# Scan of a two-block transformer kernel: local attention products as block-diagonal matmuls, values for two head pairs at a time

## What is computed

```
scores = einsum('bhnd,bhmd->bhnm', q_s, k_s) * SCALE          # rotated q, k
scores = where(mask, scores, -inf)
sdpa   = einsum('bhnm,bhmd->bhnd', softmax(scores), v_s)      # local products
num    = einsum('bhnk,bhkv->bhnv', elu1(qn_s), mem); den = ...
out    = beta * num / (den + 1e-6) + (1 - beta) * sdpa
prev_v = einsum(elu1(kn_s), mem) / ...
mem    = mem + einsum('bhnk,bhnv->bhkv', elu1(kn_s), v_s - prev_v)
```

## Time and profile before

| | us |
|---|---|
| three runs, median (lowest to highest) | 3109.3 (3105.91 to 3112.54) |
| the profiled execution, own time | 3109.39 |
| its span in the profile | 3107.6 |
| PE busy of the span | 2664.5 (86%) |
| DVE busy | 2506.4 (81%) |
| ACT busy | 1875.9 (60%) |
| POOL busy | 1758.7 (57%) |
| scan, 1700 to the end | 1407 |

### The profile page before, as it was taken

How to read it: one execution, slowest core, us unless ns; L and a number is a source line. 1 busy time by engine, 2 the same in 40 slices (tenths; PEclk the granted TensorE clock), 3 DMA queues, 4 the chain that set the end, 5 groups by cost and what they waited for, 6 DMA issues and landing times. The chain is left out here.

```text
span 3107.6 us, 129631 instructions
## 1 busy us (share of the span) xinstructions
PE 2664.5 (86%) x53553; PEld 1513.6 (49%) x53553; DVE 2506.4 (81%) x7598; ACT 1875.9 (60%) x3797; POOL 1758.7 (57%) x1988
## 2 busy tenths in 40 slices
PE   5887999999999999782331899999999998999998
PEld 2442333333333333372220666666666666666665
DVE  4677989999999999586606888888888888888887
ACT  5785999999999999630001555555455555555543
POOL 5883222222222222240063888888888888888886
PEclk9896999999999999895655999999999999999999
DMA  4676434444444443191023000000000000000000
GB/s 126 205 241 155 90 89 94 94 107 94 91 94 98 96 94 87 39 325 55 10 40 91 4 11 11 11 11 4 11 11 11 11 11 11 11 11 5 11 8 11
DMA packets 173633, 201.58 MB, mean 65 GB/s; under 512 B 31152, under 2 KB 134512, under 8 KB 172784
## 3 DMA queue, kind: packets, MB, share of 16 engines
q1 hardware_dynamic: 170480, 191.87, 23.8%
q0 software_dynamic: 2560, 1.35, 0.4%
HBM read 125.10 MB, written 67.24 MB: 62 GB/s over the span
## 5 line engine op out<-in xcount | busy, mean ns | idle before, releaser
L851 ACT ACTIVATE at_pA<-at_ps 128x512 f32<-128x512 f32 x1024 | 551.8, 614 | 57.8 <-DVE at_ps L903 51.1
L912 DVE CUSTOM_DVE_ANT_0 at_junk<-at_ps,w_cmask 128x512 f32<-128x512 f32 (+3 forms) x1024 | 463.4, 485 | 102.7 <-PE at_ps L754 95.4
L903 DVE TENSOR_TENSOR at_ps<-at_ps,w_ratio 128x128 f32<-128x128 f32 (+3 forms) x1024 | 451.2, 491 | 2.1 <-PE at_ps L748 0.5
L720 POOL TENSOR_SCALAR_AFFINE_SELECT at_pB<-at_pB 128x128 f32<-128x128 f32 x256 | 74.8, 292 | 640.4 <-ACT at_pB L857 638.3
L857 ACT ACTIVATE at_pB<-at_ps 128x512 f32<-128x512 f32 (+1 forms) x768 | 379.5, 531 | 53.0 <-PE at_ps L761 47.7
L2001 POOL TENSOR_TENSOR sc_rb<-sc_rb,v_sin 128x512 f32<-128x512 f32 x256 | 326.0, 1274 | 42.4 <-DVE sc_ra L2241 41.1
L2037 PE MATMUL sc_ps<-sc_xT,v_wqkv 128*128 128x512 f32 x512 | 287.2, 644 | 4.0 <-PEq L56 1.4
L748 PE MATMUL at_ps<-at_aq,at_ak 72*128 72x512 bf16 x1024 | 278.3, 388 | 0.2
L2200 ACT COPY sc_skN<-sc_ps 128x512 f32<-128x512 f32 x128 | 75.1, 587 | 324.8 <-PE sc_ps L2089 324.8
L1996 POOL TENSOR_TENSOR sc_sk<-sc_ee,sc_relu 128x512 f32<-128x512 f32 x128 | 165.4, 1293 | 180.8 <-ACT sc_ee L2191 180.7
L761 PE MATMUL at_ps<-at_bq,at_bk 75*128 75x512 bf16 (+3 forms) x1024 | 265.8, 302 | 1.5 <-ACT at_pB L857 0.9
(11 more groups left out here) (317 smaller groups left out, 5949.9 us busy)
## 6 DMA issues: line engine op xcount, KB each, us to landing
parts_scratch<-fr_parts SPq DMA_DIRECT2D x64, 384.0 KB, 4.1
at_bk<-parts_scratch SPq DMA_DIRECT2D x192, 96.0 KB
at_ak<-parts_scratch SPq DMA_DIRECT2D x192, 96.0 KB
v_scratch<-fr_v SPq DMA_DIRECT2D x32, 352.0 KB, 4.4
at_v<-v_scratch SPq DMA_DIRECT2D x32, 352.0 KB, 3.5
at_bq<-parts_scratch SPq DMA_DIRECT2D x128, 64.0 KB
at_aq<-parts_scratch SPq DMA_DIRECT2D x128, 64.0 KB
on_scratch<-at_on SPq DMA_DIRECT2D x32, 256.0 KB, 2.2
```

The lines of the kernel that those rows point to most:

```text
L851: act.activation(pA[:, n % A_RING, j * S:(j + 1) * S], src, ACT.Exp).then_inc(exped, 1)
L903: dve.tensor_tensor(src[:, 0:wide], src[:, 0:wide], W["ratio"][:, S - wide:S], ALU.mult).then_inc(tilted, 1)
L912: ins = dve.tensor_tensor_reduce(junk[:, P * j * (j + 1) // 2:P * (j + 1) * (j + 2) // 2], src[:, col:col + wide], W["cmask"][:, S - wide: ...
```

## The change

- `local(p)` now issues 8 matmuls instead of 32: for each `g` and head one with a 128 x 128 stationary operand `pB`, which holds the four 32 x 32 blocks on its diagonal and zeros elsewhere, and the values of all 128 partitions as the moving operand (64 columns). The four blocks' products come out in the same places of PSUM.
- `pB` is a new tile, [128, 2, 8, 4, 32], set to zero once by DVE in `prepare`. ScalarE places the blocks: `place_blocks(p)` at the start of step p+2, four copies of 32 partitions x 256 elements, from `pT` to the diagonal places, after DVE's transposition (`pt`, now given by the transposition itself) and after `local(p-2)` (`pvd`). PE waits for the last copy (`pb`). DVE's `old` waits for the reciprocal by a new semaphore `smd`, and the transposition waits for the copies of pair p-4.
- `values(s)` now computes two of the four groups `g` for two neighbouring pairs at a time: 2 matmuls with 256 moving columns instead of 4 with 128. ACT's copy (the same size) moves to both pairs' places in `uu`.
- Seven waits of PE that others imply are left out or made conditional.

```diff
--- before.py
+++ after.py
@@ -1791,6 +1791,7 @@
         rot = [sb("qr", [P, 2, S]), sb("kr", [P, 2, S])]
         GH = 2 * BG
         ss, pT = sb("ss", [P, 2, GH, SEG]), sb("pT", [P, 4, GH, SEG])
+        pB = sb("pB", [P, 2, GH, B1, SEG])
         mx, sm = sb("mx", [P, GH]), sb("sm", [P, 4, GH])
         rk, rq = sb("rk", [P, GH]), sb("rq", [P, GH])
         t1, t2 = sb("t1", [P, 2, GH, DH]), sb("t2", [P, 2, GH, DH])
@@ -1799,7 +1800,7 @@
 
 
         names = ("h_in0 h_in1 stat fact shift_d xn_d tq_d xnn_d xq_d step xt xt_c xqt xqt_c hb_d ffn ffn_c vp v_c pj ex mn rp sn sgq sgk add_d sS skt skc "
-                 "sx se pt pvd old kr_s qr_s kd ud qd od up mu ott otc oproj yt_c yt ydone stored0 stored1").split()
+                 "sx se pt smd pb pvd old kr_s qr_s kd ud qd od up mu ott otc oproj yt_c yt ydone stored0 stored1").split()
         G = {n: sem(n) for n in names}
         h_seg = c["h_d"].rearrange("(g f) (s i) d -> f s i g d", f=B1, i=SEG)
         o_seg = out.rearrange("(g f) (s i) d -> f s i g d", f=B1, i=SEG)
@@ -1909,6 +1910,7 @@
                 @block.vector
                 def _(dve):
                     link = linker(dve)
+                    dve.memset(pB[:], 0.0)
                     moments(dve, link, 0)
                     shifts(dve, 1)
                     round_fp8(dve, link, 1)
@@ -2038,9 +2040,12 @@
 
                     def values(p):
                         free_bank(pe, "v", p)
-                        col = 2048 + p % PAIRS * P
-                        for g in range(BG):
-                            ins = pe.matmul(ps[:, bank_of("v", p), g * P:(g + 1) * P], xT[:, p // PAIRS % 2, g * P:(g + 1) * P], V["wqkv"][:, col:col + P],
+                        first = p - p % 2
+                        col = 2048 + first % PAIRS * P
+                        two = ps[:, bank_of("v", p), :].rearrange("p (n g d) -> p n g d", n=2, g=2)
+                        for k in range(2):
+                            g = 2 * (p % 2) + k
+                            ins = pe.matmul(two[:, :, k], xT[:, p // PAIRS % 2, g * P:(g + 1) * P], V["wqkv"][:, col:col + 2 * P].rearrange("p (n d) -> p n d", n=2),
                                             start=True, stop=True)
                         ins.then_inc(G["vp"], 1)
 
@@ -2066,10 +2071,9 @@
                     def local(p):
                         for g in range(BG):
                             for hh in range(2):
-                                for f in range(B1):
-                                    ch = 2 * g + hh
-                                    ins = pe.matmul(ps[32 * f:32 * f + 32, 6, ch * DH:(ch + 1) * DH], pT[32 * f:32 * f + 32, p % 4, ch, :],
-                                                    uu[32 * f:32 * f + 32, p % PAIRS, g, hh, 0:DH], start=True, stop=True)
+                                ch = 2 * g + hh
+                                ins = pe.matmul(ps[:, 6, ch * DH:(ch + 1) * DH], pB[:, p % 2, ch].rearrange("p f j -> p (f j)"),
+                                                uu[:, p % PAIRS, g, hh, 0:DH], start=True, stop=True)
                         ins.then_inc(G["pvd"], 1)
 
                     def score(p):
@@ -2096,8 +2100,9 @@
 
                     def project_out(p):
                         wait(pe, "otc", p + 1)
-                        wait(pe, "yt_c", p // PAIRS)
                         h = p % PAIRS
+                        if h == 0:
+                            wait(pe, "yt_c", p // PAIRS)
                         pe.matmul(ps[:, 7, :], V["wout"][:, h], oT[:, p % 2], start=(h == 0), stop=(h == PAIRS - 1)).then_inc(G["oproj"], 1)
 
                     def turn_y(bank, j):
@@ -2113,15 +2118,13 @@
                             project(2 * s)
                         p = s - 2
                         if inside(p):
-                            wait(pe, "otc", min(s - 3, PT))
-                            wait(pe, "pt", p + 1)
+                            wait(pe, "pb", p + 1)
                             local(p)
                         if s < PT:
                             values(s)
                         p = s - 2
                         if inside(p):
                             wait(pe, "mu", 2 * min(s - 5, PT - 1) + 1)
-                            wait(pe, "sgk", p + 1)
                             recall(p, 1, "kr_s")
                         p = s - 1
                         if inside(p):
@@ -2130,7 +2133,6 @@
                             turn_keys(p)
                         p = s - 1
                         if inside(p):
-                            wait(pe, "mu", 2 * min(s - 5, PT - 1) + 2)
                             wait(pe, "add_d", 2 * p + 2)
                             score(p)
                         if s < PT:
@@ -2138,7 +2140,6 @@
                         p = s - 2
                         if inside(p):
                             wait(pe, "kd", min(s - 1, PT))
-                            wait(pe, "sgq", p + 1)
                             recall(p, 0, "qr_s")
                         p = s - 4
                         if inside(p):
@@ -2154,8 +2155,8 @@
                         p = s - 4
                         if inside(p):
                             wait(pe, "qd", min(s - 1, PT))
-                            wait(pe, "sx", min(s, PT))
-                            wait(pe, "mu", 2 * p)
+                            if s > PT + 1:
+                                wait(pe, "mu", 2 * p)
                             wait(pe, "ud", p + 1)
                             update(p)
                         for j in at_step(s, 5):
@@ -2190,7 +2191,17 @@
                         wait(act, "ex", n + 1)
                         act.activation(ee[:, which], ee[:, which], ACT.Exp, scale=-1.0).then_inc(G["mn"], 1)
 
+                    def place_blocks(p):
+                        wait(act, "pt", p + 1)
+                        wait(act, "pvd", p - 1)
+                        for f in range(B1):
+                            ins = act.copy(pB[32 * f:32 * f + 32, p % 2, :, f], pT[32 * f:32 * f + 32, p % 4])
+                        ins.then_inc(G["pb"], 1)
+
                     for s in range(STEPS):
+                        p = s - 2
+                        if inside(p):
+                            place_blocks(p)
                         if s < PT:
                             features(2 * s)
                         p = s - 1
@@ -2199,9 +2210,11 @@
                             wait(act, "up", p - 3)
                             act.copy(skN[:, p % 4].rearrange("p g r -> p (g r)"), ps[:, 6, :]).then_inc(G["skc"], 1)
                         if s < PT:
+                            first = s - s % 2
                             wait(act, "vp", s + 1)
-                            wait(act, "up", s - PAIRS + 1)
-                            act.copy(uu[:, s % PAIRS, :, :, 0:DH], ps[:, bank_of("v", s), :].rearrange("p (g h d) -> p g h d", h=2, d=DH)).then_inc(G["v_c"], 1)
+                            wait(act, "up", first + 2 - PAIRS)
+                            to = uu[:, first % PAIRS:first % PAIRS + 2, 2 * (s % 2):2 * (s % 2) + 2, :, 0:DH].rearrange("p n g h d -> p n (g h) d")
+                            act.copy(to, ps[:, bank_of("v", s), :].rearrange("p (n c d) -> p n c d", n=2, d=DH)).then_inc(G["v_c"], 1)
                         p = s - 1
                         if inside(p):
                             wait(act, "sx", p + 1)
@@ -2260,7 +2273,7 @@
                         p = s - 2
                         if inside(p):
                             wait(dve, "pvd", p + 1)
-                            wait(dve, "pt", p + 1)
+                            wait(dve, "smd", p + 1)
                             wait(dve, "ott", p - 3)
                             local = ps[:, 6, :].rearrange("p (g h d) -> p g h d", h=2, d=DH)
                             for hh in range(2):
@@ -2303,10 +2316,11 @@
                         p = s - 1
                         if inside(p):
                             wait(dve, "se", p + 1)
-                            dve.transpose(pT[:, p % 4].rearrange("p c j -> p (c j)"), ss[:, p % 2].rearrange("p c j -> p (c j)"))
+                            wait(dve, "pb", p - 3)
+                            dve.transpose(pT[:, p % 4].rearrange("p c j -> p (c j)"), ss[:, p % 2].rearrange("p c j -> p (c j)")).then_inc(G["pt"], 1)
                             s_ = sm[:, p % 4]
                             link(dve.tensor_reduce(head(s_), by_head(ss[:, p % 2]), AX.X, ALU.add))
-                            dve.reciprocal(s_, s_).then_inc(G["pt"], 1)
+                            dve.reciprocal(s_, s_).then_inc(G["smd"], 1)
                         if s - 7 in starts:
                             j = (s - 7) // PAIRS
                             wait(dve, "ffn", j + 1)
```

## The result

The changed kernel takes 3381.4 us (3371.3 to 3386.8, 4 runs) against 3109.2 (3105.9 to 3112.5, 4 runs): a ratio of 1.087, 95% interval 1.085 to 1.089, 272 us slower. The profiled execution has a span of 3380.4 us. The direction was forecast; the size, +178, and the range up to 3350, were not large enough.

A forecast was written before the change was run, and what follows sets the result against it. A loop through PE and DVE bounds the kernel: transposition to recall goes from 2.81 to 4.39 us, +202 us over 128 steps, less 15 for cover and 9 for fewer MATMULs: +178 on 3109.3, 3287 us; range 3216 to 3350.

The forecast's parts named there:

- The loop: Transposition, local, values, recalls, scores, t2, rope on PE and DVE: transposition to recall 2.81 us becomes 4.39, +202 us.
- Wide products: PE's local with 128-column weight loads: 16 x 0.111 = 1.78 us against 1.03, plus 0.11 for the exposed first load.
- the prediction's estimate: Local if weight loads and columns go one after the other: 2.62 us; as a rival 3437 us in all, chance 0.04.
- Copies: ScalarE's four block copies on the loop, spaced like exp and its next instruction: 1.38 us a step.
- the prediction's upper bound (1.65): Most the four ScalarE copies would take, from four 128-column activations with per-partition scales: 1.65 us.
- Hand-over to ScalarE: From DVE's transposition to ScalarE's first copy: 0.05 us a step, of 0.17 for both hand-overs.
- The hand-over to PE: From ScalarE's last copy to the start of local on PE: 0.12 us a step.
- Cover in the steps with rounding: In 16 steps where DVE rounds to fp8, PE came late anyway and the copies are covered: -15 us.
- Clock: Rival: PE idles longer and its clock falls in 15 fp8-rounding steps, some 3 us each: +45, 3332 us; chance 0.12.
- Fewer MATMULs: PE issues 52 of 346 MATMULs a step fewer, 15% off 58 us of idle time inside groups: -9 us.
- Values and waits: PE's values for two pairs take 0.95 us instead of 1.09, a gain of 0.14 a step; omitted waits gain 0.

The follow-up runs named there:

- run 9: Kernel before with values for two pairs, the transposition giving its own semaphore and implied waits left out, without the block diagonal part: 3082.6 us, 0.990.
- run 4: Changed kernel without ScalarE's copies: PE waits for the transposition alone and multiplies by a constant pB, softmax weights left out; wide matmuls stay: 3093.1 us, 0.993.
- run 2: Changed kernel with the 32 small local products straight from pT, still behind ScalarE's copies and the wait for them: 3222.4 us, 1.035.
- run 3: Kernel of run 2 with 16 filler MATMULs on PE ahead of its wait for the blocks: 3204.5 us, 1.034.
- run 1: Changed kernel with 16 filler bf16 MATMULs of 128 columns on PE ahead of its wait for the placed blocks: 3320.9 us, 1.067.
- run 5: Changed kernel with two of the four copies per step, blocks 2 and 3 staying zero, half of the local products left out: 3224.5 us, 1.036.

## Why the prediction was right in direction and wrong in size

The runs split the 8.7% in an order in which each kernel differs from the next in one thing. What a thing costs hangs on the order: the wide products would be 9 us and not 103 if they came ahead of the copies (runs 9 and 4).

| from, to | ratio | us |
|---|---|---|
| before, the small parts (run 9) | 1.000 to 0.990 | -32 |
| copies and the wait for them (run 2) | 0.990 to 1.035 | +141 |
| filler in PE's wait (run 3) | 1.035 to 1.034 | -4 |
| wide products, filler kept (run 1) | 1.034 to 1.067 | +103 |
| filler out, clock no longer kept up (after) | 1.067 to 1.087 | +63 |

By the steps of the prediction:

- **The loop** was right for the copies: leaving out half gave their time back and more (run 5), leaving out all gave everything back (run 4).
- **Wide products: right.** 16 x 0.111 and 0.11 for the first load were 1.89; measured 1.84, with a load every 0.112 us. The loads decide, also with 64 columns moving. The Trainium skill (TensorE: Matmul & The Clock Gate, The mechanism) says that a weight load overlaps matmuls in flight only where their row groups differ. By that `local` would have taken 2.62, the prediction's estimate; this trace disagrees.
- **Copies: mis-sized.** "3 x 0.32 + 0.42 = 1.38" is 1.64, 0.26 more, 33 us: the overlap of an exp with a following activation from PSUM was not that of these copies, and the prediction's upper bound (1.65) is what came.
- **Hand-over to ScalarE: mis-sized.** "0.05" is 0.45 in the mean, 51 us. It is 0.03 in the 67 steps in which ScalarE was free. I looked at what queues behind the copies (which cost nothing here, as forecast) and not at what stands before them: the work on the next segment's input, in 60 of 128 steps. The hand-over to PE is 0.05 for "0.12", 9 us less.
- **Cover in the steps with rounding: not there.** "-15" rested on one step with 2.46 us from the transposition to `local`. The trace of before has that in 2 of 15 such steps; their mean is 1.01, and 2.37 in the changed kernel. I took the one I looked at for all.
- **Clock: the step that failed most.** I gave it a rival's 0.12 and 45 us, tied to the 15 steps with rounding at 3 us each, and 11 us of the range. It fell 58 times, and not in those alone; run 1 puts at least 63 us on it, some 1.5 for each of the 43 falls that went. Nor is PE's idle time in each step enough by itself, as I had it: run 2 has the same and 14 falls.
- **Fewer MATMULs: mis-sized the other way.** "-9" by taking 15% off the idle time inside groups. It is not in proportion: 65.5 us became 7.2 with 15% fewer MATMULs (run 4) and 2.4 in the changed kernel, 54 us more than I took off. Nor is it their number alone: run 2 has as many as run 9 and 15.0 us of it over all groups for 54.5. Where PE waits for the copies, most of this idle time goes too.
- **Values and waits**: -16 and -9 alone, forecast -18 and 0. By the trace `values` takes 1.01 for 1.09, where 0.95 was forecast.

Put together by the means of all 128 steps: from the transposition to `local` it went from 0.86 to 2.14, 164 us, where the forecast had 0.97 x 128 - 15 = 109; `local` at the upper clock costs 104 for 96, and `values` gives back 10 for 18. That is 71 more. With 63 for the clock and 54 off for the idle time it is 178 + 71 + 63 - 54 = 258, against 272. The 14 that lack are within what the 15 falls left in run 1 would cost (90 for 63). But these terms do not simply add (the parts of run 9 alone are 44 and together 32), and that 54 us more of idle time went is read from rows and not from a run of its own: that the sum comes so near is partly luck.

## What to carry to other kernels

Where two engines pass a step to each other in a loop, a third engine put between them is not covered: one adds up its work (here 1.64 us), the hand-over to it with what stands ahead in its queue (0.45 in the mean, 0.03 where it was free) and the hand-over behind it (0.05). What stands ahead has to be looked up in all kinds of steps and not in the one on the screen. The same added work can be dear or nearly free: 0.8 us on TensorE cost 103 us of 128 steps behind the wait for the copies, and 9 without it. Merging small corner matmuls into wide ones with zeros saves instructions, not time, where fp32 weight loads of 128 columns at 0.11 us decide: 32 small products took 1.03 us, 8 wide ones 1.84. Where a change opens a wait on TensorE, the clock may fall, and then that belongs into the sum: here it fell 58 times with the wait and the wide products, 14 times with the wait alone (run 2), 4 times with the wide products alone (run 4).

## What the runs showed that I had not expected

- Two kernels whose PE waits for the same copies: with the wide products 58 falls of the clock, with the small ones 14, though PE works less in the latter. Idle time alone does not tell when the clock falls; what does, these runs leave open.
- Idle time inside PE's groups went from 65.5 to 7.2 us with 15% fewer MATMULs at nearly the same time of the scan. It comes with the pace at which instructions are used up; a cause was not tested.
- ScalarE's copies from SBUF to SBUF on 32 partitions start 0.41 us after each other at 0.40 each, without the overlap of 0.1 us that its neighbours show.
